# The shifted copies of the values in windowed attention: made by DMA from SyncE instead of VectorE

## What is computed

```python
x = x + 0.5 * ffn(layernorm(x))
x = x + mla(layernorm(x))
x = x + 0.5 * ffn(layernorm(x))

def layer(x, ...):                       # ffn: two of these
    h = shift_token(x)                   # upper 64 channels come from the token before
    q, k, v = split(h @ wqkv, 3)         # 8 heads of 64
    q, k = l2norm(q) * qs, l2norm(k) * ks
    q, k = rotary_xpos(q, k)
    # windows of 64 queries see their own 64 keys and the 64 keys of the window before
    bk, bv = look_around(k), look_around(v)
    attn = softmax(mask(8 * q @ bk.T))
    x = x + (attn @ bv) @ wo
    h = layernorm(shift_token(x)) * lg + lb
    a, g = split(h @ w1 + b1, 2)
    return x + (a * gelu(g)) @ w2 + b2
```

## Time and profile before

| | |
|---|---|
| median of 3 runs | 2463.88 us (2462.53 to 2465.33) |
| profiled execution, first to last instruction | 2459.3 us |
| the rest of the median | 4.6 us |
| DVE busy | 2183.2 us, 89% |
| PE busy | 2129.6 us, 87% |
| ACT busy | 1663.2 us, 68% |
| POOL busy | 1246.0 us, 51% |
| mean granted clock of TensorE | 0.965 of full speed |

### The profile page before, as it was taken

The page is one execution under the profiler, slowest core; times in us unless marked ns, Lnnn a source line. Parts: engine busy times, 40 slices in busy tenths (PEclk is TensorE's granted clock), DMA queues, the critical chain, the costliest instruction groups (busy, mean ns, idle before and its releaser), DMA issues. The chain is left out here.

```text
span 2459.3 us, 58228 instructions
## 1 busy us (share of the span) xinstructions
PE 2129.6 (87%) x20074; PEld 1666.7 (68%) x20074; DVE 2183.2 (89%) x5134; ACT 1663.2 (68%) x3674; POOL 1246.0 (51%) x1048
## 2 busy tenths in 40 slices
PE   2888899879997988989968988998799978898997
PEld 2677777756664777777747777777466657777776
DVE  4999999968887999999969999998688879999997
ACT  1676767648895666776726677676588846777675
POOL 3656655523224565655545565564232256565553
PEclk9999999979998999999979999999899989999999
DMA  2000000000000000000000000000000000000000
GB/s 89 1 2 2 2 2 1 2 1 1 2 1 1 1 2 2 1 2 10 6 23 2 2 1 2 2 2 1 1 2 1 1 1 1 2 2 2 6 6 10
DMA packets 12619, 12.41 MB, mean 5 GB/s; under 512 B 1397, under 2 KB 11687, under 8 KB 12327
## 3 DMA queue, kind: packets, MB, share of 16 engines
q1 hardware_dynamic: 12327, 8.63, 1.2%
HBM read 6.53 MB, written 2.10 MB: 4 GB/s over the span
## 5 line engine op out<-in xcount | busy, mean ns | idle before, releaser
L847 POOL TENSOR_TENSOR RN<-SS,mhalf 128x16 f32<-128x16 f32 x128 | 374.9, 2929 | 19.1 <-DVE SS L721 19.0
L838 POOL TENSOR_TENSOR U2B<-U,b_s 128x128 f32<-128x128 f32 x128 | 61.3, 479 | 569.7 <-DVE U L727 555.4
L539 ACT ACTIVATE PR<-bank,NMX 128x128 f32<-128x128 f32 x1024 | 290.1, 372 | 56.3 <-DVE NMX L632 51.9
L596 ACT ACTIVATE GL<-bank,b_s 114x128 f32<-114x128 f32 (+1 forms) x384 | 113.3, 366 | 251.7 <-PE bank L386 251.7
L377 PE MATMUL bank<-KT,QZ 128*64 128x128 f32 x4096 | 280.5, 279 | 0.0
L377 PEld LDWEIGHTS bank<-KT,QZ 128*64 128x64 f32 x4096 | 218.7, 137 | 70.0 <-issue 70.0
L1092 ACT ACTIVATE PL<-bank,NM 128x384 f32<-128x384 f32 (+3 forms) x512 | 255.9, 542 | 14.0 <-DVE NM L1170 11.2
L1170 DVE TENSOR_REDUCE NM<-bank 128x1 f32<-128x384 f32 (+3 forms) x352 | 217.3, 635 | 38.6 <-PE bank L1006 34.9
L386 PE MATMUL bank<-HN,w_s 128*114 128x128 f32 (+1 forms) x1536 | 222.9, 282 | 0.0
L362 PE MATMUL bank<-wqkv_h,HTH 128*128 128x512 f32 x384 | 196.9, 513 | 11.1 <-DVE HTL L707 11.0
L1015 PE MATMUL bank<-cst,PL 128*128 128x128 f32 x1280 | 200.1, 275 | 3.9 <-ACT PTL L1084 1.9
(11 more groups left out here) (159 smaller groups left out, 6238.9 us busy)
## 6 DMA issues: line engine op xcount, KB each, us to landing
X<-in_L_attn_x SPq DMA_DIRECT2D x8, 256.0 KB, 4.3
out<-X SPq DMA_DIRECT2D x8, 256.0 KB, 2.3
wqkv_raw<-in_L_ffn_wqkv SPq DMA_DIRECT2D x1, 1536.0 KB
cst<-shape_constants SPq DMA_DIRECT2D x1, 771.0 KB
w_s<-in_L_ffn_w SPq DMA_DIRECT2D x1, 682.0 KB
wo_s<-in_L_ffn_wo SPq DMA_DIRECT2D x2, 256.0 KB
w_s<-in_L_ffn_w SPq DMA_DIRECT2D x2, 114.0 KB
b_s<-in_L_ffn_b SPq DMA_DIRECT2D x1, 128.0 KB
```

The source lines that it names most:

```text
L539: last = nc.scalar.activation(PR[:, 4 * g + h, :], BK[B_S[g]][:, h * P:(h + 1) * P], ACT.Exp, bias=NMX[:, 4 * g + h:4 * g + h + 1], scale=8.0)
L847: nc.gpsimd.tensor_tensor(RN[:, u % 2, :], SS[:, :], mhalf[:, 0:2 * NH], ALU.pow).then_inc(S["rn_ok"], 1)
```

## The change

The two VectorE copies and their semaphore `va_ok` go. SyncE's program gets a loop over all units of the phase, behind the loads of `X` and the clearing of semaphores and ahead of the stores. For each unit it waits for `vb_ok`, from unit 8 on for the product with the values of unit u - 7 (`o_in`, the last reader of the half of `VA` that is overwritten), and from unit 4 on for the DMAs that used the same semaphores before; then it issues two DMAs of 64 rows of 520 floats (2,080 bytes a row, 130 KB a DMA). There are eight semaphores, `va_lo` and `va_hi` for each t. TensorE waits for these in place of `va_ok`: one wait for t = 0 and two for t = 1 to 3.

```diff
+                va_lo = [sem(f"va_lo{j}", "ffn") for j in range(4)]
+                va_hi = [sem(f"va_hi{j}", "ffn") for j in range(4)]
...
+                        sp.wait_ge(S["preset"], 5)
+                        for u in range(NU):
+                            l, bb, t, s = unit(u)
+                            sp.wait_ge(S["vb_ok"], u + 1)
+                            if u >= 2 * NT:
+                                sp.wait_ge(S["o_in"], u - 2 * NT + 2)
+                            if u >= 4:
+                                if t < NT - 1:
+                                    sp.wait_ge(va_lo[t + 1], 16 * (u // 4))
+                                sp.wait_ge(va_hi[t], 16 * (u // 4))
+                            if t < NT - 1:
+                                sp.dma_start(VA[0:W, bb, t + 1, :, :], VB[W:P, bb, t, :, :]).then_inc(va_lo[t + 1], 16)
+                            sp.dma_start(VA[W:P, bb, t, :, :], VB[0:W, bb, t, :, :]).then_inc(va_hi[t], 16)
                         if store:
...
-                                pe.wait_ge(S["va_ok"], u + 1)
+                                pe.wait_ge(va_hi[t], 16 * (u // 4 + 1))
+                                if t:
+                                    pe.wait_ge(va_lo[t], 16 * (u // 4 + 1))
...
-                            u = n - 3
-                            if live(u):
-                                l, bb, t, s = unit(u)
-                                dve.wait_ge(S["vb_ok"], u + 1)
-                                if u == 0:
-                                    dve.wait_ge(S["preset"], 5)
-                                if t < NT - 1:
-                                    nc.vector.tensor_copy(VA[0:W, bb, t + 1, :, :], VB[W:P, bb, t, :, :])
-                                nc.vector.tensor_copy(VA[W:P, bb, t, :, :], VB[0:W, bb, t, :, :]).then_inc(S["va_ok"], 1)
...
-                return list(S.values()) + x_in
+                return list(S.values()) + x_in + va_lo + va_hi
```

More of the change, by code:

```diff
@@ L303, in ffn_phase @@
                     "preset uT_in u2T_in ht_ok ht2_ok q_in k_in v_in kmul qmul ksq sq_ok ss_ok qsum_ok ksum_ok rn_ok qrot_ok krot_ok hh_ok "
-                    "qT_in kT_in qz_ok kt_ok s0_in s1_in nmx0_ok nmx1_ok p0_ok p1_ok pt0_in pt1_in pt0_ok pt1_ok vb_ok va_ok o_in on_ok "
+                    "qT_in kT_in qz_ok kt_ok s0_in s1_in nmx0_ok nmx1_ok p0_ok p1_ok pt0_in pt1_in pt0_ok pt1_ok vb_ok o_in on_ok "
                     "ot_in ot_ok wo_in u2_ok u2b_ok mean_in dt_ok sq2_ok var_in ve_ok rv_ok dg_ok bc_in hn_ok "
```

## The result

The changed kernel takes **2351.9 us** (2350.4 to 2353.6, four runs) against 2464.5 us of the kernel before on the same chip (2462.5 to 2465.3, four runs): a ratio of 0.9549 with an interval of 0.9535 to 0.9562, or 112.6 us less. The forecast was 2374 us, 89.8 us less, with a range from 2345 to 2400. The measured time lies inside that range but 6 us outside the forecast's own, 2358 to 2390: it is the room that was left for the first rival that takes it in, and that rival's mechanism isn't what happened. The sign, the place and most of the mechanism were right; the saving was put 20% too low, most of it in one term.

The account below looks back on a forecast made before the run. VectorE paces the ffn phases, TensorE having about 1.4 us in hand a step. 99.8 - 6.4 - 3.6 = 89.8 us off the median 2463.9 gives 2374 us; range 2345 to 2400, the forecast's own 2358 to 2390.

Parts of the forecast that it names:

- the first rival: Bare ffn steps: L632 goes ahead of GpSimd's L858, 0.87 us less; 2353 us, or 2283 in all steps; chance 0.13.
- The path of the copies: VectorE in ffn steps: without L783 and L784 a step loses 0.89 us; 99.8 us over 96 and 128 copies.
- The t = 3 steps: Steps whose unit lacks L783: 13.50 us against 13.93, taken as a trial of the change in small.
- GpSimd is next: Bare layer 0 steps: L853 must wait for L847, so they gain 0.66 us, not 0.89; 6.4 us given back over 28.
- The two stalls: VectorE's second row-maxima scaling (L632, 1.04 us) and `DG_` (L802, 1.17 us) stand until GpSimd pieces end; the change leaves them.
- The wait for the scores: VectorE's second row maximum (L630) starts 0.33 us late, waiting for TensorE's scores; cost nothing, as L632 still stands.
- Filling steps: First two units of each phase: copies may hide GpSimd waits; 8 pairs worth 7.1 us, half taken, 3.6 us off.
- The DMA: SyncE's 224 DMAs: estimated 2.3 us each against 29.8 us of cover, so they cost nothing in the steps.
- TensorE's clock: Rival in ffn steps: denser TensorE is granted less clock; at 0.90 it costs 30 us, 2404 us; chance 0.09.
- A stall vanishes too: Rival on VectorE's L632 in bare steps: it goes before L858, taking 0.17 us; 21 us more gain, 2353; chance 0.13.

## Why the prediction was right, and where not

**The path of the copies (99.8 us forecast, 92.7 of them in the 120 steps behind the filling): mis-sized, and the largest miss.** The prediction took 246.08 - 245.19 = 0.89 us, from the start of the first copy to the start of `VE`. It asked when the removed work began and ended. It should have asked when `VE` could start without it. In the trace of the change `VE` starts 0.08 us behind the start of the scaling ahead of it, while the first copy had stood 0.20 or 0.21 us behind that start. So the copies held the path for 246.08 - 244.98 - 0.08 = 1.02 us as a pair and 0.57 alone. The run with both copies beside the DMAs gives 1.02 again, and the run with one copy 0.58. The kernel before showed such a start too, of the row maximum behind `VE`, 246.16 - 246.08. The t = 3 steps, which the prediction took as a trial in small, couldn't show it: they still hold one copy, and with it the gap ahead of it. Over the 120 steps behind the filling, 88 x 1.02 + 32 x 0.57 = 108.0 us, where the prediction's 0.89 and 0.45 give 92.7.

**"GpSimd is next" (6.4 us given back): right in kind, a little small.** Bare steps came out at 13.22 us; 13.27 was forecast. The give-back there is 1.02 - 0.71 = 0.31 us with two copies and 0.57 - 0.27 = 0.30 with one, 8.6 us over 28 steps. In layer 1 the forecast was 13.39 with `VE` still the last, but `VE`, which comes 0.13 us earlier than thought, now ties with the power: 13.27. Moving `VE` earlier gains nothing, moving the power earlier gains 12 us and nothing in layer 1, and both together gain 73, so the tie is shown from both sides.

**The two stalls: right.** The second scaling still stands (0.82 us, ending 0.03 us behind L866's 247.95) and `DG_` takes 1.18 us. The wait for the scores, 0.33 us forecast and 0.42 measured, cost nothing, as worked out.

**Filling steps (3.5 us forecast): mis-sized, too low.** From the head of a phase to its first `U2B` it was 34.0, 35.6, 36.5 and 34.6 us and is 32.4 in each: 11.0 us. The prediction said that the copies of the first two units were worth at most their 7.1 us, since their stalls covered a GpSimd piece. In fact more than that went: six of L783 and two of L784 had taken 1.2 to 1.5 us (one stands in the earlier trace rows), 7.3 us more than eight usual ones, and these stalls were handed on only in small part. Over the four stretches VectorE's other pieces exceed their shortest times by 9.6 us before and 11.2 after; one scaling of the first phase, for instance, takes 0.61 us where it took 0.17. The prediction had the stalls as cover for GpSimd's pieces, and argued that from one row.

**The DMA: right.** It lands in 2.3 us (2.2 to 4.0), against a cover of some 29 us, and no wait for `VA` is in the list of waits. Without DMAs the steps are the same to 0.02 us. The Trainium skill (DMA: Bandwidth & Descriptors, Anatomy of one DMA) gives by its formula, which was fitted on GpSimd's path, an estimate of 2.3 us for 130 KB, and this trace agrees; for 260 KB it gives 2.6 us, and the run with fewer DMAs shows 3.2.

**The turn (not in the sum): a term that was missed.** The prediction costed SyncE's issues in the steps and its stores, and not that SyncE's program stands in an outer loop. It cost 4.3 us and hid a part of the miss above.

**TensorE's clock (rival, 0.09): wrong in direction.** The denser TensorE ran at 1.00 in the steps. The kernel before had seven steps in layer 1 of some 14.8 us instead of 14.28, each right behind a step with a mean granted clock of 0.88 or 0.89, the run with the old copies put back had several too, with spells of a lower granted clock; the change has none. Two neighbouring stretches of before:

```profile
402.00:406.00 4.00, 2.15 (x19) 1.94 (x18) 4.00 (x10) 2.33 (x8) 2.35 (x3) 0.97 0.00 0
406.00:410.00 4.00, 4.00 (x42) 3.25 (x43) 3.81 (x11) 2.77 (x4) 0.74 (x2) 0.60 0.01 4
```

TensorE was busy for 2.15 of 4 us in the first and got 0.60 on average, a mix of its levels of 2.4 and 1.2 GHz, in the second. The change is worth some 3.7 us more by these seven steps; the rival had feared a loss of 30.

**A stall vanishes too (rival, 0.13): its time, 2353, is near the measured one, its mechanism isn't there.** The scaling takes 0.82 us and not 0.17, and the steps have the length of the forecast. The two agree by chance. Even with both moves, at 2277 us, the second scaling doesn't go ahead of GpSimd's piece for 0.17 us: the stall of the scalings moves to the first, and the one that goes is that of `DG_`, which the rival didn't name.

**The account of the span.**

The 99.8 us stand in two rows, as the 92.7 of the 120 steps and the 7.1 of the filling, less the 3.6 taken off there. Of the right column, the filling and the turn are measured between the same instructions in both traces; the other three terms are worked out from single steps.

| term | forecast, us | from the traces, us |
|---|---|---|
| copies on VectorE's path, 120 steps | 92.7 | 108.0 |
| given back to GpSimd, 28 bare steps | -6.4 | -8.6 |
| filling of the pipeline, four phases | 3.5 | 11.0 |
| steps with a lower clock | 0 | 3.7 |
| turn of the outer loop | 0 | -4.3 |
| sum | 89.8 | 109.8 |
| span | | 110.6 |

Measured directly, the stretches from the first to the last `U2B` of a phase are 101.4 us shorter in all, where the three terms worked out make 103.1: some of the last steps of a phase gain nothing (one is 9.75 us before and after). Behind the last `U2B` the phases are 2.3 us shorter. With 101.4 + 11.0 + 2.3 for the phases, 3.8 lost between them and 0.3 around them, the 110.6 us are complete.

## What to carry to other kernels

A removed operation is worth what the start of its successor moves, so measure from the start of the piece ahead to the start of the piece behind, and take off the gap that this pair needs with nothing between. When two rows of work tie, as VectorE's and GpSimd's did here, an edit to either one looks worth little (0 and 12 us here, where both gave 73); try the pair. Look also at how often an engine's program turns: here 56 DMAs a phase on an idle engine cost nothing in any step and 4 us between rounds, and making two transfers into one took most of that turn back, 18.5 to 15.1 us.

## What the hardware showed that was not expected

- The start of a piece on VectorE isn't always behind the end of the piece ahead: `VE`, which reads a bank of PSUM, started 0.08 us behind the start of a scaling that lasts 0.17 us; a copy from SBUF to SBUF stood 0.20 us behind it.
- Copies of 64x520 kept their 0.42 us inside GpSimd's power of 2.94 us, as L783 does in the earlier trace rows, while scalings lasted four to six times as long beside GpSimd's pieces of 128x512, and the copies themselves 1.2 to 1.5 us beside such pieces in the filling. The Trainium skill (SBUF — State Buffer, Who interferes with whom) says that a copy of VectorE in its two-port mode and any GpSimd instruction shut each other out; in this trace that holds for the one kind of GpSimd piece and not for the other. Why wasn't tried.
- SyncE's program alone can make the turn of an outer loop longer: 14.3 to 14.5 us with none of the loop, 15.0 with 24 DMAs a phase, 15.1 with 32, 18.0 with 192 waits, 18.2 to 19.1 with 56 DMAs and their waits.
- A TensorE that waited 1.86 us in a layer-1 step of 14.3 us had spells at a lower granted clock; with 1.41 us (one copy left) and 0.85 us (none) it had none in layer 1. They go together here; whether these waits are the cause wasn't tested by themselves. The clock of layer 1's stretch, before, then with one copy left:

```profile
1551.00:1690.00 139.00, 123.56 (x1255) 102.81 (x1251) 134.07 (x319) 96.70 (x215) 83.83 (x70) 0.98 0.01 2
```

```profile
1510.00:1650.00 140.00, 126.16 (x1307) 105.27 (x1306) 135.78 (x323) 101.74 (x228) 85.42 (x72) 1.00 0.04 9
```
